# Cross attention in a Flamingo layer: turns four steps behind the scores, eight exponential blocks, the next batch's keys split over two batches

## The reference

```python
def xattn(q, k, v, mask, Wq, bq, Wk, bk, Wv, bv, Wo, bo):      # q: 32x100x256, k = v: 32x361x256
    Q, K, V = q @ Wq.T + bq, k @ Wk.T + bk, v @ Wv.T + bv       # split into 16 heads of 16
    scores = einsum('bhqd,bhkd->bhqk', Q, K) / sqrt(16)
    scores = where(mask, scores, finfo.min)
    A = einsum('bhqk,bhkd->bhqd', softmax(scores), V)
    return A @ Wo.T + bo
x = x + tanh(g_xattn) * xattn(layernorm(x), ctx, ctx, mask, ...)
x = x + tanh(g_ffn) * ffn(layernorm(x), ...)
```

## Time and profile before

| | us |
|---|---|
| median of 3 runs | 1932.85 (1931.35 to 1933.55) |
| the profiled execution | 1932.07 |
| its span, first to last instruction | 1930.3 |
| TensorE, VectorE, ScalarE, GpSimd busy | 1871.1, 1476.6, 1135.5, 951.1 |

### The profile page before, as it was taken

One profiled execution on the slowest core, in us unless ns is written; L12 is line 12 of the kernel. 1 busy time (PEld: TensorE's weight loads), 2 busy tenths in 40 slices (PEclk: granted clock), 3 DMA queues, 4 the chain that ended last, 5 costly groups with the idle time before them and its releaser, 6 DMA issues. The chain is left out here.

```text
span 1930.3 us, 57615 instructions
## 1 busy us (share of the span) xinstructions
PE 1871.1 (97%) x13454; PEld 1145.8 (59%) x13454; DVE 1476.6 (76%) x4245; ACT 1135.5 (59%) x3591; POOL 951.1 (49%) x1432
## 2 busy tenths in 40 slices
PE   5899999999997999999999999999999999999998
PEld 3688888888875555444444445545555555555543
DVE  6688888888887961555555556658999999999989
ACT  3688888888886444444444445545555555555543
POOL 4022222222212001666666666666677676776766
PEclk9999999999998999999999999999999999999999
DMA  6677888788862484000000023122222222222201
GB/s 156 122 118 117 120 119 120 118 120 119 120 88 88 202 329 188 27 27 27 14 27 27 27 82 97 50 71 66 71 80 67 79 75 72 79 70 76 75 15 64
DMA packets 192148, 174.22 MB, mean 90 GB/s; under 512 B 51921, under 2 KB 183378, under 8 KB 190034
## 3 DMA queue, kind: packets, MB, share of 16 engines
q1 hardware_dynamic: 189906, 165.06, 37.7%
q0 software_dynamic: 2176, 8.39, 1.2%
HBM read 112.41 MB, written 60.98 MB: 90 GB/s over the span
## 5 line engine op out<-in xcount | busy, mean ns | idle before, releaser
L1496 POOL TENSOR_TENSOR o_side<-o_side,o_tmp 128x256 f32 (+1 forms) x528 | 397.2, 752 | 195.8 <-POOL o_side L1496 72.8
L1265 PE MATMUL e_pv<-e_vw,e_xhi 128*128 (+1 forms) x1600 | 475.9, 379 | 1.2 <-ACT e_out L1188 1.2
L1198 ACT ACTIVATE big<-e_pv,gates 128x128 f32<-128x128 f32 x800 | 227.9, 368 | 280.8 <-PE e_pv L1265 279.3
L1624 ACT ACTIVATE o_tmp<-o_py,gates 128x256 f32<-128x256 f32 x528 | 221.8, 473 | 193.0 <-PE o_py L1696 143.8
L661 ACT ACTIVATE c_ex<-c_sm,c_nmax 100x361 f32<-100x361 f32 x512 | 302.1, 592 | 53.5 <-DVE c_nmax L554 46.2
L554 DVE CUSTOM_DVE_ANT_0 c_sm<-c_ps,c_mbias 100x361 f32<-100x361 f32 x512 | 267.4, 523 | 55.9 <-PE c_ps L746 51.2
L1696 PE MATMUL o_py<-o_whi,a_chi 128*128 128x512 f16 x800 | 304.2, 380 | 0.1
L1696 PE MATMUL o_py<-o_wlo,a_chi 128*128 128x512 f16 x800 | 303.8, 380 | 0.0
L1696 PE MATMUL o_py<-o_whi,a_clo 128*128 128x512 f16 x800 | 303.7, 380 | 0.0
L1265 PE MATMUL e_pv<-e_vw,e_xlo 128*128 (+1 forms) x800 | 303.2, 379 | 0.0
L1131 DVE TENSOR_SCALAR e_acc<-e_pv,gates 128x128 f32<-128x128 f32 x400 | 121.8, 346 | 227.5 <-PE e_pv L1265 227.4
(11 more groups left out here) (164 smaller groups left out, 3206.4 us busy)
## 6 DMA issues: line engine op xcount, KB each, us to landing
qk<-e_out SPq DMA_DIRECT2D x16, 1600.0 KB, 5.2
c_kst<-k_parts SPq DMA_DIRECT2D x256, 90.2 KB, 4.9
a_q<-qk SPq DMA_DIRECT2D x64, 200.0 KB, 2.4
a_k<-qk SPq DMA_DIRECT2D x64, 200.0 KB, 2.4
v<-e_out SPq DMA_DIRECT2D x20, 640.0 KB, 3.3
a_v<-v SPq DMA_DIRECT2D x64, 200.0 KB
c_ctx<-in_ctx_t SPq DMA_DIRECT2D x32, 361.0 KB, 3.4
e_wst<-in_v_w POOLq DMA_DIRECT2D x8, 1024.0 KB, 7.7
```

Source lines behind the costliest of these rows:

```text
L1198: act.activation(tmp[:, hh, e, :], p_v[:, hh, 1, e * PD:(e + 1) * PD], ACT.Copy, scale=gate).then_inc(s_av, 1)
L1265: last = pe.matmul(p_v[:, hh, half, :], a[:, c, bass.ds(t * P, P)], vw[:, bass.ds(col + (w * DC + c) * VW, 512)], start=j == 0, stop=j == ...
L1496: pool.tensor_tensor(side[:, x.t, :], side[:, x.t, :], tmp[:, slot(x, r), j, :], ALU.add).then_inc(s_pool, 1)
L1624: act.activation(tmp[:, slot(x, r), j, :], p_y[:, q, j, :], ACT.Copy, scale=gate).then_inc(s_av, 1)
```

## The change

LAG_T, LAG_C, LAG_E, LAG_A go from 3, 4, 3, 5 to 4, 5, 4, 6: turns, their copies and the attends come one step later after the scores. The ring of exponentials gets eight blocks (`XR`), and `exp` waits for the turn of eight heads ago. Each of TensorE's sixteen steps now holds at most one piece beside scores and turn: an attend, a piece of values or keys, or half of the projection (step 6 has values and `turn_rden`). The keys are shared between two batches: the first block of batch b + 2 in steps 14 and 15 of batch b, the second block of batch b + 1 in steps 0 and 2 of batch b (not in batch 0, where the start phase has made both). So `stack_keys(b + 1)` runs in body b of SyncE, where `stack_keys(b + 2)` did. `key_hi` and `key_lo` of the second block go to step 3. `invert` stays in step 2; `normalize`, `residual`, `moments`, `mean_var` go from 7, 11, 12, 13 to 8, 13, 14, 15, `copy_rt` from 6 to 7, the evacuations of values from 4, 6, 9 to 5, 8, 11.

```diff
+XR = 8
...
-    LAG_T, LAG_C, LAG_E, LAG_A = 3, 4, 3, 5
+    LAG_T, LAG_C, LAG_E, LAG_A = 4, 5, 4, 6
...
-                if later(b, 2):
-                    stack_keys(later(b, 2))
+                if not is_first(b) and later(b, 1):
+                    stack_keys(b.next())
...
-                    if i == 15 and later(b, 2):
-                        key_lo(later(b, 2), 0)
-                    if i == 0 and not is_first(b) and later(b, 1):
-                        key_lo(later(b, 1), 1)
+                    if i in (1, 3) and not is_first(b) and later(b, 1):
+                        key_lo(later(b, 1), i // 2)
...
-                    if i == 7 and not is_first(b):
+                    if i == 8 and not is_first(b):
                         normalize(b.before())
-                    if i == 11 and not is_first(b):
+                    if i == 13 and not is_first(b):
                         residual(b.before())
-                    if i == 12 and not is_first(b):
+                    if i == 14 and not is_first(b):
                         moments(b.before())
-                    if i == 13 and not is_first(b):
+                    if i == 15 and not is_first(b):
                         mean_var(b.before())
...
-                at_least(act, s_t, XH * b.n + h - 3)
-                act.activation(ex[:, h % 4, 0:SK], sm[:, h % 4, :], ACT.Exp, scale=-1.0,
+                at_least(act, s_t, XH * b.n + h - XR + 1)
+                act.activation(ex[:, h % XR, 0:SK], sm[:, h % 4, :], ACT.Exp, scale=-1.0,
...
-                    if i == 15 and later(b, 2):
-                        key_hi(later(b, 2), 0)
-                    if i == 0 and not is_first(b) and later(b, 1):
-                        key_hi(later(b, 1), 1)
-                    if i == 6 and not is_first(b):
+                    if i in (0, 3) and not is_first(b) and later(b, 1):
+                        key_hi(later(b, 1), i // 3)
+                    if i == 7 and not is_first(b):
                         copy_rt(b.before())
-                    if i == 4 and not is_last(b):
-                        values(b.next(), 0)
+                    if i in (5, 8, 11) and not is_last(b):
+                        values(b.next(), (5, 8, 11).index(i))
                     exp(b, i)
-                    if i in (6, 9) and not is_last(b):
-                        values(b.next(), (4, 6, 9).index(i))
...
-            ahead = {1: (1, values, 0, 0), 2: (1, values, 0, 1), 3: (1, values, 1, 0), 5: (1, values, 1, 1),
-                     7: (1, values, 2, 0), 9: (1, values, 2, 1),
-                     11: (2, keys, 0, 0), 13: (2, keys, 0, 1), 14: (2, keys, 1, 0), 15: (2, keys, 1, 1)}
-            behind = {5: (turn_rden,), 10: (project_all,)}
+            ahead = {0: (1, keys, 1, 0), 2: (1, keys, 1, 1),
+                     3: (1, values, 0, 0), 4: (1, values, 0, 1), 6: (1, values, 1, 0), 7: (1, values, 1, 1),
+                     8: (1, values, 2, 0), 10: (1, values, 2, 1),
+                     14: (2, keys, 0, 0), 15: (2, keys, 0, 1)}
+            behind = {6: (turn_rden,), 11: (project, 0), 12: (project, 1)}
...
-    c.ex = m.sbuf("c_ex", [SQ, 4, SKP])
+    c.ex = m.sbuf("c_ex", [SQ, XR, SKP])
```

More of the change, by code:

```diff
@@ L753, in turn @@
                     last = pe.transpose(p_t[0:KW, h % 2, c * SQ:(c + 1) * SQ],
-                                        ex[:, h % 4, c * KW:(c + 1) * KW], k.ident[0:SQ, 0:SQ])
+                                        ex[:, h % XR, c * KW:(c + 1) * KW], k.ident[0:SQ, 0:SQ])
                 last.then_inc(s_t, 1)
@@ L795, in project @@
                     last.then_inc(s_o, 1)
-            def project_all(b):
-                for c in range(DC):
-                    project(b, c)
             def start(n):
@@ L818, in start, with due @@
                               stop=True).then_inc(s_bo, 1)
-            ahead = {1: (1, values, 0, 0), 2: (1, values, 0, 1), 3: (1, values, 1, 0), 5: (1, values, 1, 1),
-                     7: (1, values, 2, 0), 9: (1, values, 2, 1),
-                     11: (2, keys, 0, 0), 13: (2, keys, 0, 1), 14: (2, keys, 1, 0), 15: (2, keys, 1, 1)}
-            behind = {5: (turn_rden,), 10: (project_all,)}
+            ahead = {0: (1, keys, 1, 0), 2: (1, keys, 1, 1),
[3 more added lines that the diff above has]
+            behind = {6: (turn_rden,), 11: (project, 0), 12: (project, 1)}
+            def due(b, i):
+                return i in ahead and later(b, ahead[i][0]) and not (i in (0, 2) and is_first(b))
             def body(b):
@@ L827, in body @@
                     scores(b, i)
-                    if i in ahead and later(b, ahead[i][0]):
+                    if due(b, i):
                         n, work, *args = ahead[i]
```

## The result

The change makes the kernel slower: 1979.73 us median of 4 runs (1978.43 to 1981.47) against 1932.1 for the kernel before in the same session, a ratio of 1.0247 with an interval of [1.0229, 1.0265]. The profiled execution of the change has a span of 1979.0 us at a mean granted clock of 0.985.

A forecast was written before the change was run, and what follows sets the result against it. TensorE was taken to set the pace, at 16.27 us a batch with some waits. A ring of 16.9 us over 30 batches gave +18.9, less 0.9 and 0.5: +17.5, so 1950 us, range 1938 to 1971.

The forecast's parts named there:

- the main term: Moved keys, written to DRAM and read back before the next step 0: 16.9 us a batch, +18.9 us over 30.
- the forecast's own sum: Over the whole kernel: ring +18.9, keys leaving batch 0 -0.9, last batch -0.5, all else nothing: +17.5 us.
- the rival on the clock: TensorE's steps 0 to 3 run at 1.2 GHz after each wait: 120 us more, 2070; chance 0.03.
- The ring's links: From step 0 to the keys' write 4.85 us, from write to last stacked read's landing 11.8: 16.65 a batch.
- quarter of a microsecond: Added to the links' row sum for semaphore hops, TensorE's refill and SyncE's queue, giving 16.9 us a batch.
- Just clear: On SyncE's queue, the context load lands at 5.4 us, before the key write moves data from about 5.7.
- Small terms: Outside the ring: keys leaving batch 0 -0.9 us, the last batch -0.5, evacuations, Gpsimd and memset nothing.
- A batch would take 14.9 us: TensorE's sixteen steps sum to 14.92 us, a batch's time if looser lags won back every wait.
- The lags do nothing: Rival: copies still follow turns by a step, a batch without the ring stays at 16.3; also 1950; no chance given.
- Fewer waits on the row maximum: Sign of being right: TensorE's loads for scores wait less on the row maximum; no size given.
- The rule on a DMA's time: Skill's 2.0 us fixed plus bytes gives 2.2 us a stacked read, no binding ring, about 1902; forecast followed the rows instead.

The follow-up runs named there:

- experiment 4: The change with eight matmuls of no use ahead of TensorE's wait at step 0, from batch 2 on: 1964.51 us, 1.0167 to the kernel before.
- experiment 5: The change with the keys' high part ahead of ScalarE's copy in step 3: 1994.27 us, 1.032 to the kernel before.
- experiment 3: The change with SyncE's context load moved behind the stacked reads: 1970.48 us, 1.0197 to the kernel before.
- the best run: The change with keys one batch further ahead, context loaded a batch earlier and split before the mask is widened, new lags, eight blocks: 1915.43 us, 0.9914.
- experiment 9: The change, keys one batch further ahead, context loaded earlier and split before mask widening: 1915.43 us; the same with old lags and four blocks: 1941.78.
- experiment 1: New lags and eight blocks with the old table and old keys, turn_rden, normalize and copy_rt one step later: 1958.63 us, 1.0132 to the kernel before.
- experiment 6: The change with context load behind the stacked reads and keys' high part ahead of the copy: 1947.07 us; with eight idle matmuls too: 1947.72.

## Why the prediction was wrong

The sign and the mechanism of the main term held: the moved keys close a ring over DRAM, TensorE waits at step 0 in all 30 batches (52.4 us, 40 to 65 forecast), and what the lags free goes into that wait. The size did not: +17.5 forecast, +47.6 measured, outside the range. With the undisturbed ring in every batch the forecast's own sum gives 30 x 17.23 - 488.15 - 1.4 = +27.35, some 1960 and inside it; what the sum put at nothing took it out.

- **The step that failed** is the rival on the clock, which was given one price, 120 us for a fall in every batch, and a chance of 0.03, and so no share in the sum. It happened in part: waits of 1.2 to 3.8 us at step 0 left the clock at 1.00 in most batches and at 0.5 in some. The five batches without another disturbance that had a fall cost 8.0 us, batch 2 another 2.8, and the fall at 614.9 goes with 2.9 more behind batch 31's step 0; keeping TensorE busy gave back 15.2 in all (experiment 4). Row 98:99 showed one idle microsecond without a fall, which bears on one wait and not on thirty. The Trainium skill (TensorE: Matmul & The Clock Gate, HAM oscillation) tells of a kernel throttled in each turn of a loop by its waits for DMA; these runs show it in some turns, five of the thirty beside the disturbed ones, and in every second batch from batch 20 of experiment 5, each behind a wait of 3.3 to 3.7 us.
- **Not foreseen, and so also at nothing:** disturbances of the key write that the slack of the kernel before hid. The late writes of batches 1, 2, 28 and 29 cost 5.3 us, those of batches 8 and 12 another 1.7.
- **The ring's links.** Undisturbed, it takes 17.23, not 16.9. Step 0 to write measured 4.98 to 5.07 instead of 4.85; write to last landing 12.1 on average (2.65 to the first read, 9.45 from there) instead of 11.8, of it at most 0.2 by the context load (2.47 to the first read in experiment 3); landing to step 0 another 0.13. The "quarter of a microsecond" for the last of these and all else came from no row and was too small: all the links were a little longer than their rows, none shorter. This is 30 x 0.33 = 10 us. "Just clear", of the context load, was wrong: SyncE issued it 0.7 us later than forecast.
- **Small terms.** Batch 1 starts 0.66 us earlier (0.9 forecast); what follows step 0 of batch 31 takes 2.9 us more (1363.34 against 1360.48) instead of 0.5 less, as told above.
- **The lags' worth.** "A batch would take 14.9 us" if every wait were won back: the best run took 15.5. The rows of the sum left out `turn_rden`, whose step takes 1.01 in the best run, and an attend of 1.42 (step 5), and half a projection takes 0.89. It did not enter the sum. "The lags do nothing" fell: they are worth 26 us in experiment 9. But what they win back is not the wait that was named. "Fewer waits on the row maximum" was a sign of being right, and it failed: 24.8 us of PEld in the change against 11.9, and 23.9 in the best run, where the same kernel with the old lags has none. The waits that went are those for copies of turned blocks, for the keys' low part and on issue.
- **The rule on a DMA's time.** Landings of the stacked reads stayed at 3.1 to 6.5 us, much as the rows of before had it. By the rule of the Trainium skill (DMA: Bandwidth & Descriptors, Anatomy of one DMA) they would have been 2.2, an estimate; that section fits its rule to transfers that GpSimd issues, and SyncE issues these. No run shows 2.2.

## What to carry to other kernels

Before a piece of work is moved closer to its use, walk from its start through every engine and transfer back to the next start: if that walk is longer than the period, it is the period, and each link then pays its own disturbances, which slack hid before. A wait of TensorE can have a second price beside its length, a lower clock, and here it fell on the work just behind the wait. Looser lags pay only where the table of pieces fits them and transfers have a batch of room: the same lags cost 26 us in one table (experiment 1) and won 26 in another (experiment 9).

## What was not expected of the hardware

- Equal waits did not lower the clock equally: with waits of 1.2 to 3.8 us at step 0 of 30 batches, only some brought a fall to 1.2 GHz; one of 1.7 did (batch 25), one of 2.5 did not (batch 13). Five of the seven falls began 0.4 to 1.7 us after step 0, when TensorE was already at work again, and so fell on the links of the ring; two (99.5 and 614.9) began in the wait.
- A shorter link made the kernel slower (1994.27 against 1979.73), because it put a write of 180.5 KB right behind a context load of 361 KB, and the first read came 4.8 us behind the write instead of 2.5.
- Two instruction packets, 0.03 MB together, in the time of a write of 180.5 KB go with a landing after 3.8 instead of 2.5 us; where packets came 2 us behind the write (experiment 6), it landed after 2.4 to 2.5.
